# Two VectorE steps of the front swapped, and the last merge of each attention stage moved from GpSimd to VectorE

## What is computed

```
x0 -> xn = layernorm(x0)
      s  = attention0(xn)            16 heads, 128 plain + 64 rotary dims, values of 128, output @ Wo.T
      g  = silu(ffn0(xn))            ffn0 = down(silu(gate(xn)) * up(xn)), 704 hidden, integer weights with a scale per row
      x1 = x0 + s * g
x1 -> xn = layernorm(x1)
      s  = attention1(xn)            16 heads of 16 dims, rms norm of q and k, projection with a bias
      g  = silu(moe(xn))             8 experts of 176, the best 2 of each token, and a shared one of 352
      x2 = x1 + s * g
```

## Time and profile before

| | |
|---|---|
| median of 3 runs | 1444.42 us (1443.23 to 1447.38) |
| the profiled execution | 1444.3 us |
| its span, first to last instruction | 1442.4 us |
| PE busy | 1369.1 us, 95% |
| DVE, ACT, POOL busy | 64%, 57%, 53% |
| mean granted clock of PE | 0.983 |

### The profile page before, as it was taken

The page is one execution under the profiler, slowest core; times in us unless marked ns, Lnnn a source line. Parts: engine busy times, 40 slices in busy tenths (PEclk is TensorE's granted clock), DMA queues, the critical chain, the costliest instruction groups (busy, mean ns, idle before and its releaser), DMA issues. The chain is left out here.

```text
span 1442.4 us, 25701 instructions
## 1 busy us (share of the span) xinstructions
PE 1369.1 (95%) x8880; PEld 1225.2 (85%) x8880; DVE 917.6 (64%) x1781; ACT 821.8 (57%) x2172; POOL 766.3 (53%) x759
## 2 busy tenths in 40 slices
PE   6988899999999999999999998799999999999996
PEld 5876689998899889998999987688889988889896
DVE  6554565656566665656566665467777778777754
ACT  4543455455544655445544453178787778777873
POOL 1543234445343545434544443477669676767864
PEclk9999899999999999999999999799999999999999
DMA  5887333233431343233423334135224242432442
GB/s 174 276 279 271 78 98 94 67 93 115 108 87 48 105 138 86 65 88 99 114 85 87 111 86 147 52 125 153 75 92 120 76 147 82 117 117 90 140 133 73
DMA packets 85681, 165.64 MB, mean 115 GB/s; under 512 B 16720, under 2 KB 27664, under 8 KB 83248
## 3 DMA queue, kind: packets, MB, share of 16 engines
q1 hardware_dynamic: 85552, 163.99, 37.5%
HBM read 99.90 MB, written 22.09 MB: 85 GB/s over the span
## 5 line engine op out<-in xcount | busy, mean ns | idle before, releaser
L750 POOL TENSOR_TENSOR a_pr<-a_pr,a_ri 128x512 f32<-128x512 f32 x128 | 133.4, 1042 | 305.0 <-DVE a_ri L930 304.7
L807 ACT ACTIVATE a_pr<-a_score,a_nb 128x256 f32<-128x256 f32 x256 | 119.2, 471 | 269.1 <-DVE a_nb L922 269.1
L1281 POOL TENSOR_TENSOR l_pr<-l_pr,l_ri 128x512 f32<-128x512 f32 x128 | 133.5, 1043 | 123.5 <-DVE l_ri L1651 122.6
L1409 ACT ACTIVATE l_pr<-l_score,l_nb 128x256 f32<-128x256 f32 x256 | 119.2, 471 | 81.4 <-DVE l_nb L1622 80.6
L55 PE MATMUL a_job<-s_xs,s_wh 128*128 128x512 f32 x384 | 156.1, 406 | 5.1 <-PEq L204 5.1
L56 PE MATMUL a_job<-s_xs,s_wh 128*128 128x512 f32 x384 | 152.4, 397 | 0.0
L57 PE MATMUL a_job<-s_xs,s_wl 128*128 128x512 f32 x384 | 151.9, 396 | 0.0
L922 DVE TENSOR_REDUCE a_nb<-a_score 128x2 f32<-128x512 f32 x128 | 88.5, 691 | 88.8 <-PE a_score L993 88.8
L1622 DVE TENSOR_REDUCE l_nb<-l_score 128x2 f32<-128x512 f32 x128 | 87.5, 684 | 36.8 <-PE l_score L1748 36.3
L935 DVE TENSOR_TENSOR a_pt<-a_turn,a_pt 128x512 fp32r<-128x512 f32 x128 | 87.4, 683 | 24.4 <-ACT a_pt L815 24.4
L1772 PE MATMUL l_out<-s_wh,l_vp 128*128 128x256 f32 x512 | 92.5, 302 | 0.9 <-DVE s_wh L1626 0.9
(11 more groups left out here) (239 smaller groups left out, 4809.1 us busy)
## 6 DMA issues: line engine op xcount, KB each, us to landing
s_wl<-wgu_scratch SPq DMA_DIRECT2D x56, 512.0 KB, 4.7
a_sk<-a_rotk SPq DMA_DIRECT2D x384, 64.0 KB, 2.0
a_sq<-a_rotq SPq DMA_DIRECT2D x256, 64.0 KB, 2.0
s_xs<-xn_scratch SPq DMA_DIRECT2D x14, 1024.0 KB, 5.7
l_wd<-wd_scratch SPq DMA_DIRECT2D x56, 256.0 KB, 2.7
a_raw<-in_w SPq DMA_DIRECT2D x30, 256.0 KB, 3.0
wgu_scratch<-f_split SPq DMA_DIRECT2D x14, 512.0 KB, 4.6
f_praw<-in_moe_w SPq DMA_DIRECT2D x14, 384.0 KB, 3.5
```

Source lines behind the costliest of these rows:

```text
L750: pool.tensor_tensor(e, e, ri[:, n % 2, :].unsqueeze(2).broadcast_to([P, 2, SEQ]), ALU.mult)\
L807: i = act.activation(pr[:, n % 2, t, :], PS[n % 2][:, t * SEQ:(t + 1) * SEQ], ACT.Exp, bias=nb[:, n % 2, t:t + 1], accum_out=sm[:, n % 2, ...
L1281: pool.tensor_tensor(e, e, ri[:, n % 3, :].unsqueeze(2).broadcast_to([P, 2, SEQ]), ALU.mult)\
L1409: i = act.activation(pr[:, n % 3, t, :], PS[n % NPS][:, t * SEQ:(t + 1) * SEQ], ACT.Exp, bias=nb[:, n % 3, t:t + 1], accum_out=sm[:, n % 3 ...
```

## The change

In `stage_first`, at k = 1, `y_sum(si - 1)` is issued on DVE before `norm_x(si + 1)`. This concerns steps 1 and 2, where both exist.

In `stage_attention0`, the merge of the last output job, `o1` of the last round, is no longer on POOL. DVE does it, after its last slot, with the same two operations. SP waits for seven merges.

In `stage_layer1`, the merge of the second half of the last step is no longer on POOL. DVE does it after its last slot, and the last store waits on a new semaphore.

```diff
@@ stage_first, DVE @@
                         if k == 1:
-                            norm_x(si + 1)
                             if si >= 1:
                                 y_sum(si - 1)
+                            norm_x(si + 1)
@@ stage_attention0, SP @@
-                sp.wait_ge(S["merged"], 2 * NSTEP)
+                sp.wait_ge(S["merged"], 2 * NSTEP - 1)
@@ stage_attention0, POOL @@
-                        if merges(job):
+                        if merges(job) and job != ("o1", NST - 1):
                             merge(job[1], int(job[0][1]))
@@ stage_attention0, DVE, after the last slot @@
+                last = NSTEP * TT - 2
+                at = extra(NST - 1, 1, 0) % NRAW
+                xg = [raw[:, at + j, :].rearrange("p (t d) -> p t d", t=2) for j in range(2)]
+                for j in range(2):
+                    dve.wait_ge(raw_in[at + j], 16 * (extra(NST - 1, 1, j) // NRAW + 1))
+                dve.wait_ge(S["job_free"], JOB["o1", NST - 1] + 1)
+                own(dve.tensor_tensor(sacc[:, last:, :], sacc[:, last:, :], xg[1], ALU.mult))
+                own(dve.tensor_tensor(sacc[:, last:, :], sacc[:, last:, :], xg[0], ALU.add))
@@ stage_layer1, SP, store @@
-                        sp.wait_ge(S["merged"], 2 * s + i + 1)
+                        if (s, i) == (NSTEP - 1, 1):
+                            sp.wait_ge(S["last_merged"], 1)
+                        else:
+                            sp.wait_ge(S["merged"], 2 * s + i + 1)
@@ stage_layer1, POOL, after the last slot @@
-                for i in range(2):
-                    gate_out(NSTEP - 1, i)
-                    merge(NSTEP - 1, i)
+                gate_out(NSTEP - 1, 0)
+                merge(NSTEP - 1, 0)
@@ stage_layer1, DVE, after the last slot @@
+                last = NT - 2
+                yy = y[:, 1, :].rearrange("p (t d) -> p t d", t=2)
+                dve.wait_ge(S["y_act"], 2 * NSTEP)
+                wait_free(dve, ("P1", BATCH - 1))
+                own(dve.tensor_tensor(yy, yy, s1[:, (NSTEP - 1) % 2, 2:4, :], ALU.mult))
+                dve.tensor_tensor(x1[:, last:, :], x1[:, last:, :], yy, ALU.add).then_inc(S["last_merged"], 1)
```

More of the change, by code:

```diff
@@ L1150, in stage_layer1 @@
             "pv_done", "out_hi", "out_free", "tanh_ready", "gate_done", "cmul", "hid_hi", "hid_lo", "down_done",
-            "lg_exp", "cm_ready", "y_ready", "y_tanh", "y_act", "gated", "merged", "stored")}
+            "lg_exp", "cm_ready", "y_ready", "y_tanh", "y_act", "gated", "merged", "last_merged", "stored")}
         def wait_free(engine, item):
```

## The result

The changed kernel took 1433.18 us in the median of 6 runs (1432.24 to 1434.12), the kernel before 1443.83 beside it (6 runs, 1440.12 to 1447.78). The ratio is 0.9923, with a 95% interval of 0.9905 to 0.9942. Forecast were 1433.1 and a range of 1430.6 to 1438.5. Run twice more, on two chips, the changed kernel gave 1435.33 (5 runs, ratio 0.9953, 0.9936 to 0.9970) and 1437.2 (10 runs, 0.9952, 0.9933 to 0.9972). All 21 runs together have a median of 1435.1, and the 63 of the kernel before 1442.9: 7.8 us, not 10.7 (8.3 between the two means). So the first comparison was on the generous side, and the changed kernel is faster in each of the three.

What follows compares the result with a forecast made beforehand. PE was taken as the bound, busy eight or nine tenths nearly everywhere. Front 8.6 (6.5 waits + 3.4 clock - 1.3 given back), hand-over 1.55 and last merge 1.2 sum to 11.35 us: 1444.42 to 1433.1, range 1430.6 to 1438.5.

Steps and rivals of the forecast that it cites:

- The two waits: Front, steps 1 and 2: PE's waits of 2.79 and 3.75 us for the sums of y go, 6.5 us.
- The clock: Front, behind the two waits: without PE's idle time the granted clock does not fall, 1.7 + 1.7 = 3.4 us.
- Given back in the tail: End of the front: fuller DMA engines take back 1.3 of 9.9 us, leaving 8.6.
- a full DMA queue and its buffers: Front's tail: DMA share reaches the 0.95 that the same queue and buffers reached in the last 30 us.
- What is late next: Front: the normalisation becomes late next, with xn ready 1.5 us (step 1) and 0.4 us (step 2) before PE asks.
- The 0.4 us to spare in step 2: Front, step 2: xn ready at 84.8, PE asks at 85.2; new wait bounded by 0 and 1 us, taken as 0.
- the 3.9 us of the 128x256 group: Front, step 2: duration of the normalisation's 128x256 operations on DVE, counted as 3.9 us when placing xn.
- rival C: Front: the stall is not removed, normalisation or sums hold PE; only the merges' gains stay, 1441.7 us; chance 0.05.
- The hand-over: End of first attention stage: last merge on DVE ends at 910.1, gaining 1.55 us, bounds 0.3 and 1.7.
- the whole of it is gained: Hand-over to the second layer: all engines meet before the next stage, so all 1.55 us reach the total.
- The last merge: End of the kernel: two DVE operations replace GpSimd's before the store, gaining 1.2 us, bounds 0.1 and 1.4.
- The total: Whole kernel: 8.6 + 1.55 + 1.2 = 11.35 us gained, from median 1444.42 to 1433.1 us; chance 0.60.

Runs made afterwards that it cites:

- e4: Kernel before, order unchanged, plus 19 and 26 extra PE transposes ahead of its 2.79 and 3.75 us waits for sums of y; 1442.02 us, ratio 0.9989.
- e3: Kernel before with only the kernel's last merge moved from GpSimd to DVE; 1443.71 us, ratio 1.0000.
- e7: Changed kernel plus 40 PE transposes at the end of the front and 22 at the end of the first attention stage; 1432.83 us.
- e6: Changed kernel with a fourth buffer for the front's split weight pieces (NSPLIT 3 to 4); 1434.03 us.
- e8: Changed kernel with 2.9 us of extra DVE statistics between the sums of y and the normalisation in steps 1 and 2; 1437.33 us.
- e1: Kernel before with only the front's swap (sums of y ahead of the normalisation), both merges still on GpSimd; 1435.64 us, ratio 0.9935.
- e9: Changed kernel with a fourth split buffer and extra PE transposes at the two block ends; 1429.42 us, ratio 0.9902.
- e5: The changed kernel run again unaltered, with a second profile; 1435.33 us, ratio 0.9953.

## Why the prediction was right

- **The two waits.** 6.5 us forecast, and both are gone. The sums start 0.02 us behind the gated product (forecast: within 0.2), and PE's unbroken work from 48 to 100 us is as forecast.
- **The clock.** 3.4 us forecast, 3.5 to 3.9 measured alone (e4). The prediction gave each wait its own fall of 1.7 us. In the mean that is right, one by one it is not: in e3's profile, with the same waits of 2.80 and 3.75 us, the clock did not fall behind the first and fell for longer around the second, where 0.54 over 6.8 us is a loss of 3.1 us (busy us of each engine, clock, DMA share, GB/s):

```profile
54.40:62.40 8.00, 7.95 (x51) 7.18 (x52) 3.30 (x5) 4.29 (x7) 3.84 (x3) 1.00 0.96 328
84.20:91.00 6.80, 6.73 (x23) 5.89 (x24) 1.88 (x3) 1.96 (x3) 1.82 (x1) 0.54 0.58 196
```

- **Given back in the tail.** 1.3 us forecast. The four executions with the swap, three buffers and nothing added end the front at 127.05 us in the mean, the five without it at 135.9: 8.9 us gained of 9.9, so 1.0 given back. With e7, whose front is the same up to its end, it is 127.4, and 1.4 given back. The forecast for the front was 8.6. e6 shows the cause, which the prediction had put on a full DMA queue and its buffers together: the buffers.
- **What is late next.** The 0.4 us to spare in step 2 were 0.6 in the changed kernel (xn at 79.89, the transposes at 80.52), but they were read as work of DVE. The prediction took the 3.9 us of the 128x256 group as the work of the group; the same group takes 1.38 where GpSimd is not at work, so 2.5 us of it is standing beside GpSimd. DVE can do 2.84 us more there and PE feels nothing of it (e8), so rival C was further off than it looked.
- **The hand-over.** 1.55 forecast, 1.44 measured there, but the step "the whole of it is gained" failed. The mean gain after the ramp is 0.2 us, because the second layer's first 40 us run on a clock that moves by more than that.
- **The last merge.** 1.2 forecast, 1.2 measured (5.3 against 4.1 in every execution).
- **The total.** 11.35 forecast, 10.65 in the first comparison, 7.8 over all runs (8.3 between the means). That the forecast 1433.1 met 1433.18 is luck in part: it starts from 1444.42, the median of three runs, 1.5 us above that of all 63, and the two later samples of the changed kernel gave 1435.3 and 1437.2. The parts as measured are 8.9 + 0.2 + 1.2 = 10.3, or 9.9 with e7. What makes this into 8 is settled only in part.
- **The rest of the total.** In the runs of before beside e1 to e4 the fastest, 1439.71 us, had a mean granted clock of 0.985 and one of 1450.03 had 0.976: so from one execution to the next the time moves by as much as the change is worth. With 21 and 63 runs the means are known to 0.5 and 0.4 us, so a part of the gain is probably lost in the later stages. The clock points to it: its mean is 0.9825 in the 57 runs of before that stand with their clocks, and 0.9825 in the 21 of the changed kernel, though the swap takes away falls worth 3.4 of 1443 us, 0.0024. So on average the clock fell about as much more elsewhere; these two means are known to 0.0003 and 0.0004. In the profiles the stretch behind the ramp, from the first attention tile of the second layer to the 22nd behind it, took 80.5 to 80.6 us in four of five executions with the merge on GpSimd and 81.2 to 81.7 in six of seven with it on DVE. That is one fall of the clock: in the window from 112 to 122 us behind the start of the third block it was granted 0.83 in every one of the long executions (e9 too) and 1.00 in every short one (e7 too), and PE has no idle time ahead of it. Whether it follows the merge, one in five against seven in nine, or chance, was not tried.

## What to carry to other kernels

An in-order engine that frees a bank for PE should do that first and the work that nobody waits for yet second; the price of the wrong order here was PE's wait and half as much again for the clock behind it. Before counting a step at a block boundary as gained, look at what the clock does in the next 40 us, over several executions: 1.4 us were in every trace, and none of it could be found in the time. And where PE must idle, cheap matmuls into a free bank kept its clock at 1.00 (e4, and the start of the attention stage in e9): with one more buffer they brought 5.7 us over all runs of the changed kernel, 7.8 over those beside it.

## What was not expected of the hardware

A DVE operation on 128x4 took 1.75 us in place of 0.17 while GpSimd subtracted, and statistics on 128x256 did not stretch beside the same GpSimd work (e8).

The clock also fell where PE had no idle time. Two windows of the changed kernel, and behind them one of its repetition (e5) at the program's place of the second; PE is busy in all three:

```profile
1011.00:1016.00 5.00, 5.00 (x47) 5.00 (x45) 3.37 (x8) 3.64 (x11) 4.53 (x10) 1.00 0.22 88
1016.00:1021.00 5.00, 5.00 (x32) 5.00 (x32) 2.13 (x7) 1.74 (x6) 2.78 (x7) 0.66 0.00 0
```

```profile
1014.00:1019.00 5.00, 4.94 (x43) 4.77 (x43) 3.28 (x11) 2.98 (x9) 2.58 (x6) 1.00 0.00 0
```

The same kernel was granted 0.66 in one execution and 1.00 in another. This is the fall named under the total above. It costs 0.6 to 1.2 us each time (81.2 to 81.7 against 80.5), and it is one source of the scatter.
